# Attention scores by contractions of 32 rows in four banks, in a decoder kernel on one core

## What is computed

```python
scores = jnp.einsum('bhqd,bhkd->bhqk', q, k) / jnp.sqrt(jnp.float32(dk))
attn = jax.nn.softmax(scores, axis=-1)
out = jnp.einsum('bhqk,bhkd->bhqd', attn, v)
out = out.transpose(0, 2, 1, 3).reshape(B, S, D)
return out @ Wo.T + bo
```

## Time and profile before

| | |
|---|---|
| median of 3 runs | 1755.0 us (1753.84 to 1756.11) |
| profiled execution | 1753.96 us |
| its span, first to last instruction | 1752.2 us |
| TensorE busy | 1632.9 us, 93% |
| VectorE, ScalarE, POOL busy | 76%, 75%, 52% |
| TensorE's mean granted clock | 0.973 |

### The profile page before, as it was taken

One profiled execution on the slowest core, in us unless ns is written; L12 is line 12 of the kernel. 1 busy time (PEld: TensorE's weight loads), 2 busy tenths in 40 slices (PEclk: granted clock), 3 DMA queues, 4 the chain that ended last, 5 costly groups with the idle time before them and its releaser, 6 DMA issues.

```text
span 1752.2 us, 48756 instructions
## 1 busy us (share of the span) xinstructions
PE 1632.9 (93%) x12187; PEld 1349.9 (77%) x12188; DVE 1324.5 (76%) x4216; ACT 1309.1 (75%) x3583; POOL 914.6 (52%) x2450
## 2 busy tenths in 40 slices
PE   6997699999998999989999999999999999489997
PEld 4775588888885444447888888888888888389997
DVE  5887588788786778776788788789999999534443
ACT  6995588888886778787888888888888888323332
POOL 3552455545542343334555545566888888634443
PEclk9998799999999999998999999999999999789999
DMA  7990000000000000000000000011111111167875
GB/s 198 403 395 3 13 14 12 13 12 12 13 11 1 0 0 0 0 0 1 1 0 0 0 0 1 12 26 25 35 37 35 37 34 35 66 174 232 234 231 152
DMA packets 85209, 108.17 MB, mean 62 GB/s; under 512 B 33682, under 2 KB 62501, under 8 KB 85102
## 3 DMA queue, kind: packets, MB, share of 16 engines
q1 hardware_dynamic: 80494, 98.01, 18.1%
q0 software_dynamic: 4320, 8.53, 1.4%
q10 hardware_dynamic: 288, 0.34, 0.1%
HBM read 63.18 MB, written 44.12 MB: 61 GB/s over the span
## 4 chain that ended last, share of the span: by engine, by line
PE 58%; DVE 9%; issue 7%; ACT 6%; POOL 6%; DMA 1%; DVEq 0%; ACTq 0%; SPq 0%; POOLq 0%
PE sx_ps_o L1171 16%; PE sx_ps_s L1104 9%; PE sx_ps_pt L1074 9%; PE sx_ps_y L1165 4%; PE sx_ps_s L1487 4%; PE sx_ps_pt L1491 3%; PE sx_ps_j L1133 2%; PE sx_ps_j L1135 2%; PE sx_ps_j L1134 2%; PE sx_ps_y L1499 2%; PE sx_ps_o L1499 2%; DVE sx_on L832 2%; ACT ffn_gr L1291 1%; DVE sx_pr L804 1%; POOL sx_km L967 1%
## 5 line engine op out<-in xcount | busy, mean ns | idle before, releaser
L1171 PE MATMUL sx_ps_o<-sx_vb,sx_pt 128*128 128x96 f32 x3072 | 371.0, 274 | 0.0
L1171 PEld LDWEIGHTS sx_ps_o<-sx_vb,sx_pt 128*128 128x128 f32 x3072 | 360.2, 193 | 0.0
L997 ACT ACTIVATE sx_pt<-sx_ps_pt 128x512 f32<-128x512 f32 x384 | 208.6, 595 | 110.1 <-PE sx_ps_pt L1074 110.0
L798 DVE TENSOR_REDUCE sx_mx<-sx_ps_s 128x8 f32<-128x512 f32 x384 | 247.3, 685 | 17.5 <-PE sx_ps_s L1104 11.6
L967 POOL TENSOR_TENSOR sx_km<-sx_kt,const_sb 128x256 f32<-128x256 f32 x384 | 228.5, 616 | 50.0 <-ACT sx_kt L1011 47.2
L804 DVE TENSOR_TENSOR sx_pr<-sx_ps_s,sx_mx 128x512 f32<-128x512 f32 x384 | 245.2, 679 | 0.6 <-PE sx_ps_pt L1074 0.5
L991 ACT ACTIVATE sx_pr<-sx_pr 128x512 f32<-128x512 f32 x384 | 220.8, 622 | 5.8 <-DVE sx_pr L804 1.4
L1104 PE MATMUL sx_ps_s<-sx_km,sx_qm 64*128 64x256 f32 x1536 | 214.5, 399 | 8.7 <-POOL sx_km L967 8.7
L1074 PEld LDWEIGHTS sx_ps_pt<-const_sb,sx_pr 128*128 128x128 f32 x1536 | 166.2, 142 | 62.9 <-issue 62.6
L1074 PE MATMUL sx_ps_pt<-const_sb,sx_pr 128*128 128x128 f32 x1536 | 211.2, 281 | 0.0
L401 POOL TENSOR_TENSOR sx_ln_ve<-sx_ln_mv,sx_ln_eps 128x1 f32<-128x1 f32 x192 | 36.2, 189 | 335.0 <-DVE sx_ln_mv L394 323.6
(11 more groups left out here) (253 smaller groups left out, 3819.4 us busy)
## 6 DMA issues: line engine op xcount, KB each, us to landing
exp_w1b<-in_L_ffn_w_dram SPq DMA_DIRECT2D x71, 512.0 KB, 3.8
x_sorted<-no_row SPq DMA_DIRECT2D x1, 34320.0 KB, 95.3
sx_cn<-in_ctx_dram SPq DMA_DIRECT2D x128, 64.0 KB, 1.8
exp_xg<-x_sorted SPq DMA_DIRECT2D x71, 66.0 KB, 2.7
sx_mi<-in_mask_BxSxS_ik_dram SPq DMA_DIRECT2D x128, 32.0 KB
out_dram<-exp_y,exp_token POOLq DMA_INDIRECT x71, 4.4
x_sorted<-x_sb,place POOLq DMA_INDIRECT x64, 2.4
x_sb<-in_x_dram SPq DMA_DIRECT2D x1, 512.0 KB, 5.2
```

Of the source, the lines that this page charges most:

```text
L798: nc.vector.tensor_reduce(mx[:, 8 * hf:8 * hf + 8], scores_of(hf), axis=AX.X, op=ALU.max).then_inc(s["max_done"], 1)
L997: nc.scalar.activation(pt[:, 512 * hf:512 * hf + 512], ps_pt[hf][:, :], ACT.Copy).then_inc(s["pt_sb"], 1)
L1171: last = nc.tensor.matmul(ps_o[:, 2 * VW * g:2 * VW * g + av_w], pt[:, P * g:P * g + P], vb[(r + 1) % RING][:, 2 * VW * g:2 * VW * g + av_ ...
```

## The change

It makes the scores in four parts of 32 rows (two pairs of heads), each in a bank of its own, in place of two of 64 rows; K is repeated for `NPQ` = 2 pairs in place of four. The scores so take four banks. The transposed weights are left with one bank, which the two halves use in turn; the output projection moves to the bank of the transposes, the transposed attention output and the router logits to the bank of attention times values, the rank counts to that of the projections. The order of the work on TensorE and ScalarE changes with it: the second half of the weights' transposes stands behind the projections, and its copy behind that of K; the transposes of t+5 stand directly behind the first half; their copy, now into two buffers in turn, stands ahead of that of the attention output. The feed-forward and the experts get other banks.

```diff
-NPH = NPAIR // 2
-HALF = P // 2
+QUARTER = P // 4
+NPQ = NPAIR // 4
...
-        xct = sb("xct", [P, 3 * P])
+        xcts = [sb(f"xct{i}", [P, 3 * P]) for i in range(2)]
...
-        km = sb("km", [P, 2, NPH, S])
+        km = sb("km", [P, 2, NPQ, S])
...
-        ps_s = ctx.enter_context(nc.psum_tensor(f"{tag}_ps_s", [P, 2, 512], F32))
-        ps_pt = [ps("pt0"), ps("pt1")]
-        ps_m, ps_j, ps_o, ps_y = ps("m"), ps("j"), ps("o"), ps("y")
+        ps_s = ctx.enter_context(nc.psum_tensor(f"{tag}_ps_s", [P, 4, 512], F32))
+        ps_pt, ps_m, ps_j, ps_o = ps("pt"), ps("m"), ps("j"), ps("o")
+        ps_y = ps_m[:, 3 * P:4 * P]
...
                     def scores_of(hf):
-                        return ps_s[:, hf, :].rearrange("p (c x) -> p c x", x=S)
+                        return ps_s[:, 2 * hf:2 * hf + 2, 0:256].rearrange("p j (c x) -> p j c x", x=S)
...
+                    def weights(hf):
+                        act.wait_ge(s["pt_done"], 2 * t + 3 + hf)
+                        wait(act, s["av_done"], t + 1)
+                        nc.scalar.activation(pt[:, 512 * hf:512 * hf + 512], ps_pt[:, :], ACT.Copy).then_inc(s["pt_sb"], 1)
+
                     if live(t + 1):
...
+                        weights(0)
...
+                    if live(t + 5):
+                        act.wait_ge(s["t_done"], t + 6)
+                    if routed(t - 2, seg):
+                        act.wait_ge(s["rt_done"], n - 1)
+                    if hi > lo:
+                        nc.scalar.activation(xcts[(r + 1) % 2][:, lo:hi], ps_m[:, lo:hi], ACT.Copy).then_inc(s["xct_sb"], 1)
                     if live(t):
                         act.wait_ge(s["ot_done"], t + 1)
...
+                    if live(t + 1):
+                        weights(1)
+                    if live(t + 4):
+                        wait(act, s["s_done"], 4 * t + 16)
                         q_in = ps_j[:, 0:P].rearrange("p (b q) -> p b q", b=2)
...
-                        wait(pe, s["pt_sb"], 2 * t + 1 + hf)
+                        wait(pe, s["pt_sb"], 2 * t + 2 + hf)
...
-                            for hf in range(2):
-                                rows = slice(HALF * hf, HALF * hf + HALF)
-                                nc.tensor.matmul(ps_s[:, hf, :].rearrange("p (g c) -> p g c", g=4),
+                            for j in (0, 2, 1, 3):
+                                rows = slice(S * (j // 2), S * (j // 2) + S)
+                                nc.tensor.matmul(ps_s[:, j, 0:256].rearrange("p (g c) -> p g c", g=NPQ),
...
                         for b in range(2):
-                            for hf in range(2):
-                                rows = slice(HALF * hf, HALF * hf + HALF)
+                            for j in range(4):
+                                rows = slice(QUARTER * j, QUARTER * j + QUARTER)
                                 last = nc.tensor.matmul(
-                                    ps_s[:, hf, :].rearrange("p (g b c) -> p g b c", g=4, b=2)[:, :, b, :],
+                                    ps_s[:, j, 0:256].rearrange("p (g b c) -> p g b c", g=NPQ, b=2)[:, :, b, :],
                                     qm[rows, b, :, :].rearrange("p h c -> p (h c)"), km[rows, b, :, :],
...
                     if live(t + 1):
                         weights_t(0)
-                        weights_t(1)
+                    if live(t + 5):
+                        pe.wait_ge(ln["normed"], t + 6)
+                        wait(pe, s["xct_sb"], t + 5)
+                        wait(pe, s["x_done"], t)
+                        last = nc.tensor.transpose(ps_m[:, 0:P], xn[:, :], ident)
...
+                    if routed(t - 2, seg):
+                        pe.wait_ge(s["rxn"], n - 1)
+                        wait(pe, s["xct_sb"], t + 5)
+                        wait(pe, s["x_done"], min(t, total))
+                        nc.tensor.transpose(ps_m[:, 2 * P:3 * P], xn2[:, :], ident).then_inc(s["rt_done"], 1)
                     if live(t):
                         pe.wait_ge(s["on_done"], t + 1)
...
+                    if live(t + 1):
+                        weights_t(1)
                     if live(t):
                         pe.wait_ge(s["ot_sb"], t + 1)
-                        wait(pe, s["x_done"], t)
-                        nc.tensor.matmul(ps_y[:, 0:D], ot[:, :], at(t, seg).w[:, 3, :], start=True, stop=True).then_inc(s["y_done"], 1)
+                        if live(t + 5) or routed(t - 2, seg):
+                            pe.wait_ge(s["xct_sb"], t + 6)
+                        nc.tensor.matmul(ps_y, ot[:, :], at(t, seg).w[:, 3, :], start=True, stop=True).then_inc(s["y_done"], 1)
...
+                        for i in range(NPAIR):
+                            if i % 4 == 0:
+                                pe.wait_ge(s["pt_sb"], 2 * t + 3 + i // 4)
```

More of the change, by code:

```diff
@@ L1001, in body @@
                         wait(act, s["y_done"], t)
-                        nc.scalar.activation(ot[:, :], ps_y[:, P:2 * P], ACT.Copy).then_inc(s["ot_sb"], 1)
+                        nc.scalar.activation(ot[:, :], ps_ot, ACT.Copy).then_inc(s["ot_sb"], 1)
+                    if grouped(t, seg) and r == 3:
+                        act.wait_ge(s["l_done"], 8 * g)
+                        wait(act, s["order"], 16 * (g - 2) + 1)
+                        nc.scalar.activation(lg[:, :, :].rearrange("p t e -> p (t e)"), ps_l, ACT.Copy).then_inc(s["lg_sb"], 1)
                     if live(t + 4):
@@ L1022, in body @@
                                                  ACT.Copy).then_inc(s["v_sb"], 1)
[L1023 to L1027, removed]
+                    if grouped(t, seg) and r == 5:
+                        act.wait_ge(s["ranks"], g)
+                        nc.scalar.activation(rk[:, :], ps_r, ACT.Copy).then_inc(s["rk_sb"], 1)
                     if live(t + 3):
@@ L1111, in body @@
                         weights_t(0)
-                        weights_t(1)
+                    if live(t + 5):
[3 more added lines that the diff above has]
+                        last = nc.tensor.transpose(ps_m[:, 0:P], xn[:, :], ident)
+                        if at(t + 5, seg).ctx_in is not None:
+                            pe.wait_ge(s["ctx_in"], 16 * (t + 6 - (nt if isinstance(t, int) and t + 5 >= off else 0)))
+                            last = nc.tensor.transpose(ps_m[:, P:2 * P], cn[:, :], ident)
+                        last.then_inc(s["t_done"], 1)
@@ L1117, in body @@
                                             ident).then_inc(s["ot_done"], 1)
[L1118 to L1125 removed]
+                    if grouped(t, seg) and r == 5:
+                        pe.wait_ge(s["order"], 16 * (g - 1) + 8)
+                        wait(pe, s["v_sb"], 2 * min(t + 4, total))
+                        nc.tensor.matmul(ps_r[:, 0:rank_w], trib[:, 0, :], hotb[:, :, :].rearrange("p t e -> p (t e)"),
+                                         start=True, stop=False)
+                        for d in range(1, GROUP):
+                            nc.tensor.matmul(ps_r[:, d * E:rank_w], trib[:, 1, :],
+                                             hotb[:, 0:GROUP - d, :].rearrange("p t e -> p (t e)"), start=False, stop=d == GROUP - 1)
+                        nc.tensor.matmul(ps_r[:, rank_w:rank_w + E], trib[:, 1, :], hs[:, :], start=True,
+                                         stop=True).then_inc(s["ranks"], 1)
@@ L1126, in body @@
+                    if r == 6 and grouped(t, seg):
+                        wait(pe, s["rk_sb"], g)
                     if live(t + 4):
@@ L1148, in body @@
-                    if r == 6 and grouped(t, seg):
-                        wait(pe, s["rk_sb"], g)
-                    if live(t + 5):
-                        pe.wait_ge(ln["normed"], t + 6)
-                        wait(pe, s["xct_sb"], t + 5)
-                        last = nc.tensor.transpose(ps_m[:, 0:P], xn[:, :], ident)
-                        if at(t + 5, seg).ctx_in is not None:
-                            pe.wait_ge(s["ctx_in"], 16 * (t + 6 - (nt if isinstance(t, int) and t + 5 >= off else 0)))
-                            last = nc.tensor.transpose(ps_m[:, P:2 * P], cn[:, :], ident)
-                        last.then_inc(s["t_done"], 1)
@@ L1166, in body @@
+                    if routed(t - 3, seg):
+                        pe.wait_ge(s["xct_sb"], t + 5)
+                        if r == 3 and grouped(t, seg):
+                            wait(pe, s["lg_sb"], g)
+                        slot = E * ((r + 5) % GROUP)
+                        nc.tensor.matmul(ps_l[:, slot:slot + E], xcts[r % 2][:, 2 * P:3 * P], k.router_w[:, :], start=True,
+                                         stop=True).then_inc(s["l_done"], 1)
                     if live(t + 1):
-                        pe.wait_ge(s["pt_sb"], 2 * t + 4)
@@ L1322, in body @@
                 pe.wait_ge(left["v_sb"], 2 * nt)
[L1323 removed]
+            if isinstance(t, int) and t == -3:
                 pe.wait_ge(left["sub_done"], 2 * nt)
```

95 lines of the change are left out of this document (28 added, 67 removed).

## The result

The changed kernel takes 1713.6 us (median of 4 runs, 1712.25 to 1714.11) against 1755.1 of the kernel before (four runs; the 1755.0 above is of three): a ratio of 0.9765, 95% interval 0.9753 to 0.9777. The prediction had the sign and the loop right and the size wrong: it expected 1738, with 1720 as the low end, and the gain is 41.5 us in place of 17. The profiled execution took 1712.25 us, its span is 1710.4.

A forecast was written before the change was run, and what follows sets the result against it. TensorE (93% busy) with a ScalarE wait paced the kernel; a new loop without scores would follow. Gains of 2.2, 9.2 and 4.2 us in first, second and third attention, 15.6 off 1753.96, gave 1738.4 us; range 1720 to 1765.

The forecast's parts named there:

- The new loop in A and B: First and second attention: ScalarE's normalisation, TensorE's transposes, projections and second half, back to ScalarE; 5.21 and 5.10 us a tile.
- the new loop lets a fifth through: Attention tiles: of the 0.44 us a tile the scores save, 84 us in all, a fifth becomes gain.
- TensorE's part of the loop: First attention, from the end of ScalarE's normalisation to the end of the second half of the weights' transposes: 1.71 us.
- Two exponentials 1.17: ScalarE's part of the new loop: its two exponentials take 1.17 us before the normalisation of 0.48.
- I add 0.05 a tile: TensorE's restart after a stall, passing waits in its sequencer: 0.05 us more a tile, bounds 0 and 0.20.
- the bound of 0: Lower bound of TensorE's restart cost a tile; with it the sum was 1730 us.
- the three sums: Predicted loop lengths with restart: 5.21 us in the first attention, 5.10 in the second, 5.49 in the third.
- my 0.03 x 8: First attention: longer tiles among each eight add 0.03 us a tile, kept unchanged from the kernel before.
- The four tiles in eight with grouped routing steps are VectorE's: Third attention: VectorE, 92% busy, sets these tiles, so they stay; about 38 other tiles gain 0.11 us each, 4.2 us.
- Keys: POOL's instructions shrink from 616 ns to about 310; nobody waits in first and second attention, the third's mask-matmul wait of 10.3 us goes.
- The switch between mask and scores: Third attention: changing from 64-row to 32-row parts costs 0.15 to 0.18, 11 us if on the path; taken as covered.
- The linear attention, the feed-forward and the experts keep their instructions: Stages outside the three attentions: no change of time predicted, 0 us.

The follow-up runs named there:

- experiment 2: Changed kernel with its new order and banks, but scores again in two 64-row parts and keys masked for 4 pairs: 1733.9 us, ratio 0.9886 to the kernel before.
- experiment 4: Changed kernel with keys masked for 4 pairs again, of which the 32-row scores read the first 2: 1734.3 us, ratio 0.9876 to the kernel before.
- Experiment 1: Changed kernel with ScalarE's normalisations ahead of its exponentials in place of behind them: 1699.6 us, ratio 0.9687 to the kernel before.
- experiment 5: Changed kernel with the loops of the first and second attention written out, without branch or register: 1707.9 us, ratio 0.9737 to the kernel before.
- the other lost 7: Changed kernel with only TensorE's transpose of the attention output moved behind the three projections: 1721.5 us, ratio 0.9806 to the kernel before.
- experiments 7 and 8: Changed kernel with normalisations ahead of exponentials and the output transpose behind the projections: 1671.9 us; the same with first and second attention's loops written out: 1678.0 us.

## Why the prediction was wrong in size

- *The new loop in A and B*: right. It sets the pace, it starts at the normalised tile that ScalarE makes last, and scores don't lie on it: experiment 2 lengthened them by 0.41 us and A grew by 0.02 us a tile. That "the new loop lets a fifth through" of the scores' saving was even too kind: in A and B hardly any of it arrives, and what is gained there is the order's, which had taken the scores out of the loop.
- *TensorE's part of the loop*: right. 1.71 us predicted, 402.07 - 400.34 = 1.73 measured.
- *"Two exponentials 1.17"*: the first step that failed. I took the distance from the first exponential to the next instruction of the kernel before, 408.67 - 407.50. That next instruction was a copy from the accumulator memory, and starts 0.02 us behind the end of the exponential. The normalisation that follows now starts 0.09 before that end: 1.06. This is 0.11 us in each of 192 tiles, 21 us at most.
- *"I add 0.05 a tile" for the restart*: the second. In plain tiles of A the bound of 0 held. Take 0.16 off the three sums, and 5.21, 5.10 and 5.49 become 5.05, 4.94 and 5.33; the traces have 5.06, 4.95 (B with its loop written out; 5.035 in the loop) and 5.34. So the model was right in all three stages, and two terms were too long. What the loop costs shows where I didn't look: behind the branch, where A loses 0.6 us in eight tiles in place of my 0.03 x 8.
- *"The four tiles in eight with grouped routing steps are VectorE's"* and "stay": the third. They fell by 1.1 to 1.5 us in eight, and went back with the keys' old length alone (experiment 4). A mean of 92% busy over the stretch didn't say who ends a tile; the wait for the keys in 27 of some 32 tiles did, and I read it for the plain tiles only.
- *Keys*: right that the wait goes and that A and B don't notice. "About 310" ns is 399.
- *The switch between mask and scores, "I take it as covered"*: right, by little. The chain of a plain tile of C, and behind it ScalarE's normalisation for the router:

```profile
1257.57 1.81 PE sx_ps_o L1180 x16
1259.38 0.33 PE sx_ps_s L1102 x4
1259.70 0.66 PE sx_ps_s L1109 x16
1260.36 0.59 PE sx_ps_pt L1082 x4
...
1261.05 0.11 PE sx_ps_m L1124
1261.16 0.17 PE sx_ps_m L1130
...
1262.91 1.81 PE sx_ps_o L1180 x16
```
```profile
1260.47 0.48 ACT L1063 ACTIVATE sx_route_xn<-x_sb,sx_route_shift,sx_route_mv 128x128 f32<-128x128 f32 x1
```

Mask and scores take 0.33 + 0.66 = 0.99 us for 0.66 of column steps, where the scores alone in A take 0.66 for 0.44: 0.11 us more for the added switch. The Trainium skill's "TensorEngine Tiling (Array Packing)", Key Properties, says that a change of the tiling mode drains TensorE. The trace agrees: 0.11 us of TensorE a tile, where the price from rows was 0.17. But it does not lengthen the plain tile: the transpose of the router's copy (L1130) still comes 0.06 us late, as the normalisation ends at 1260.47 + 0.48 = 1260.95. Experiment 1, which makes that copy earlier, has 5.27 us, TensorE's own sum. So the foreseen loop sets C's plain tiles too, but only 0.07 us above TensorE's own sum, the next bound.
- *"The linear attention, the feed-forward and the experts keep their instructions"*: true, yet the stretch from A to B is 6.1 us shorter. Of it 4.0 lie inside the feed-forward: one tile in four takes 3.60 us in place of 3.72, and one near the end 4.31 in place of 6.70, where it shares the engines with the next attention. But experiments 2 and 5 have the same feed-forward in the same banks and show 3.72 and 3.70 again. So the banks aren't the cause; what is stays open. The stretch behind C varied from 246.0 to 253.4 us between profiles, in kernels that don't differ there (the largest in experiment 4), so single profiles tell nothing below some 5 us there.

Of the 26 us between forecast and profile 13 lie in C (the keys in the grouped tiles, and the loop's two terms), 10 in A and B (the two terms, less what the branch took back) and 6 between A and B, against 3 lost behind C.

## What to carry to other kernels

Price an engine's round by the distance between the same pair of instructions in the same order; when the follower changes, look for another place of the trace with the new pair. When a chain is broken, write down the next loop with its length before counting the gain: here, with two loops 0.04 us apart, one edit alone gained 14 us and the other lost 7, and both together gained 41. Slack on TensorE counts from its last issue, not from the end of its last result.

## What the hardware showed that was not expected

- On ScalarE the distance between two instructions depends on the pair. An exponential of 128x512 is followed after 0.52 to 0.54 us by another or by a normalisation, which starts some 0.09 before its end, but only after 0.64 by a copy from the accumulator memory. Whether the source or the number of waits decides, no run here tells.
- The sixteen records of the scores, of 32 rows and 128 columns, start within 0.46 us: four at a time within 0.03, and the fours 0.22, 0.11 and 0.11 us apart.
- POOL's product of 128 columns takes 399 ns, that of 256 takes 616: half the columns save a third.
- The loops cost 4.6 us in A and 4.5 in B where TensorE stalls in every tile (experiment 5), and nothing in their paces where it doesn't (experiments 7 and 8). How much of it is the branch, and how much the waits for values from the loop's register, was not separated.
